# Row sums of the softmax in two attentions: added on GpSimd and VectorE instead of multiplied with ones on TensorE

## What is computed

```
q, k, v = (x_norm @ Wq.T + bq), (ctx @ Wk.T + bk), (ctx @ Wv.T + bv)     # split into 16 heads of 8
scores  = einsum('bhqd,bhkd->bhqk', q, k) / sqrt(8)                      # layer 1: rotated q and k
scores  = where(mask, scores, -inf or -1e9)                              # causal, or a given mask
probs   = softmax(scores, axis=-1)                                       # exp(s - max) / row sum
out     = einsum('bhqk,bhkd->bhqd', probs, v) @ Wo.T + bo
x       = x + tanh(gate) * out
```

## Time and profile before

| | us |
|---|---|
| median of three runs (lowest, highest) | 1851.87 (1851.81, 1856.1) |
| the profiled execution | 1866.66 |
| its span in the profile | 1864.9 |
| layer 1's attention, in the span | from 654 to 912 |
| layer 3's attention, in the span | from 1373 to 1639 |
| TensorE busy, whole span | 1600.8 (86%) |
| VectorE busy | 1219.1 (65%) |
| ScalarE busy | 1218.5 (65%) |
| GpSimd busy | 745.6 (40%) |

### The profile page before, as it was taken

The page is one execution under the profiler, slowest core; times in us unless marked ns, Lnnn a source line. Parts: engine busy times, 40 slices in busy tenths (PEclk is TensorE's granted clock), DMA queues, the critical chain, the costliest instruction groups (busy, mean ns, idle before and its releaser), DMA issues. The chain is left out here.

```text
span 1864.9 us, 38943 instructions
## 1 busy us (share of the span) xinstructions
PE 1600.8 (86%) x12723; PEld 1194.1 (64%) x12723; DVE 1219.1 (65%) x3299; ACT 1218.5 (65%) x4236; POOL 745.6 (40%) x719
## 2 busy tenths in 40 slices
PE   8399999699999699999699956999768999939994
PEld 6255555499999466666589855545545666626994
DVE  4699999688888577666567756212456777753444
ACT  3399999499999378778577743433247878822444
POOL 2355675245555421121068736001321334351452
PEclk9699999899999799999899977899779999966997
DMA  5320000300000124233190021200034453331224
GB/s 167 118 80 1 1 1 1 92 4 2 1 2 1 44 84 102 74 89 90 51 326 29 1 91 62 71 0 1 1 94 120 111 153 106 84 126 39 70 72 160
DMA packets 67239, 126.85 MB, mean 68 GB/s; under 512 B 11246, under 2 KB 29921, under 8 KB 65113
## 3 DMA queue, kind: packets, MB, share of 16 engines
q1 hardware_dynamic: 57338, 104.58, 19.8%
q10 hardware_dynamic: 5328, 11.01, 1.8%
q0 software_dynamic: 4384, 8.89, 1.4%
HBM read 90.91 MB, written 49.39 MB: 75 GB/s over the span
## 5 line engine op out<-in xcount | busy, mean ns | idle before, releaser
L1660 ACT ACTIVATE L_E<-L_sc,L_negm 128x128 f32<-128x128 f32 x1024 | 299.2, 402 | 112.8 <-DVE L_negm L1519 100.7
L616 ACT ACTIVATE B_E<-B_logits,B_m 128x32 f32<-128x32 f32 (+1 forms) x1792 | 362.6, 371 | 9.3 <-DVE B_m L585 8.2
L622 POOL TENSOR_TENSOR B_E<-B_E,B_r 128x512 f32<-128x512 f32 x256 | 267.5, 1046 | 230.5 <-DVE B_r L604 230.4
L1519 DVE TENSOR_REDUCE L_negm<-L_sc 128x4 f32<-128x512 f32 x256 | 174.6, 685 | 77.9 <-PE L_sc L1771 68.9
L585 DVE TENSOR_REDUCE B_m<-B_logits 128x16 f32<-128x512 f32 (+1 forms) x256 | 173.1, 676 | 38.6 <-PE B_logits L576 31.6
L1769 PE MATMUL L_sc<-KS,L_QS 128*128 128x512 f32 x256 | 141.7, 554 | 46.5 <-ACT L_E L1660 18.2
L599 DVE TENSOR_REDUCE B_r<-B_E 128x16 f32<-128x512 f32 (+1 forms) x256 | 172.6, 674 | 2.4 <-POOL B_E L622 1.3
L1668 ACT ACTIVATE L_PT<-L_pt 128x512 f32<-128x512 f32 x256 | 166.3, 651 | 0.5 <-PE L_pt L1779 0.5
L574 PE MATMUL B_logits<-B_phihi,B_xhi 128*128 128x512 f32 x256 | 154.0, 602 | 5.5 <-ACT B_E L616 2.7
L1779 PE MATMUL L_pt<-ident,L_E 128*128 128x128 f32 x1024 | 157.1, 277 | 0.8 <-ACT L_PT L1668 0.8
L1779 PEld LDWEIGHTS L_pt<-ident,L_E 128*128 128x128 f32 x1024 | 124.0, 142 | 22.9 <-issue 1.1
(11 more groups left out here) (360 smaller groups left out, 3566.9 us busy)
## 6 DMA issues: line engine op xcount, KB each, us to landing
route_rows<-in_F_fill SPq DMA_DIRECT2D x33, 516.0 KB, 19.8
KS<-L_ksplit SPq DMA_DIRECT2D x168, 64.0 KB
L_QS<-L_qsplit SPq DMA_DIRECT2D x42, 256.0 KB
F_xg<-route_rows SPq DMA_DIRECT2D x71, 64.5 KB
ew<-in_expert_w SPq DMA_DIRECT2D x1, 4096.0 KB, 17.2
L_cT<-in_ctxT SPq DMA_DIRECT2D x16, 256.0 KB, 4.7
F_w<-in_F_w SPq DMA_DIRECT2D x2, 2048.0 KB
F_yl<-F_y_rows SPq DMA_DIRECT2D x16, 256.0 KB, 5.8
```

Of the source, the lines that this page charges most:

```text
L616: ins = nc.scalar.activation(e[:, cols], self.bank(k)[:, cols], ACT.Exp, bias=self.m[:, k % 4, g:g + 1])
L622: self.st.nc.gpsimd.tensor_tensor(e, e, self.r[:, k % 2, :].unsqueeze(2) .to_broadcast([128, self.ng, self.size]), ALU.mult).then_inc(self ...
L1519: nc.vector.tensor_reduce(negm[:, k % 4, :], sc[k % 2][:].rearrange("p (h k) -> p h k", h=NHG), AX.X, ALU.max, negate=True).then_inc(s["ma ...
L1660: ins = nc.scalar.activation(e[:, h * 128:(h + 1) * 128], sc[k % 2][:, h * 128:(h + 1) * 128], ACT.Exp, bias=negm[:, k % 4, h:h + 1])
```

## The change

TensorE's four products with `OZ` per unit go, and `OZ` with them. In their place:

- `halve(k)`, GpSimd, even units: three additions that fold E's 128 keys a head to 64, 32 and 16 columns (outputs of 256, 128 and 64 columns), each waiting for the one before.
- `add_up(k-2)`, VectorE, right behind `maximum(k)`: for odd units a reduction of all of E (128 x 512), for even ones of the 64 folded columns. ScalarE's `exponent(k)` now also waits for `sum_done` of unit k-4.
- `invert(b)` moves to the head of unit 4b + 6: reciprocal of 128 x 16 sums and a copy that widens them to 128 x 128. `spread_sums(b)`, TensorE, one transpose in unit 4b + 7. `move_ratio(b)`, VectorE, copies it out of PSUM in unit 4b + 8, and `divide(b)` multiplies as before.
- GpSimd's order is written anew, unit by unit.

The diff, without the lines that only name tiles and semaphores:

```diff
@@ GpSimd
+            def halve(k):
+                e, i = E[k % 4][:].rearrange("p (h k) -> p h k", h=NHG), k // 2
+                g.wait_ge(s["exp_done"], k + 1)
+                nc.gpsimd.tensor_tensor(fold1[:], e[:, :, 0:64], e[:, :, 64:128], ALU.add).then_inc(s["half1"], 1)
+                g.wait_ge(s["half1"], i + 1)
+                nc.gpsimd.tensor_tensor(fold2[:], fold1[:, :, 0:32], fold1[:, :, 32:64], ALU.add).then_inc(s["half2"], 1)
+                g.wait_ge(s["half2"], i + 1)
+                if i >= 2:
+                    g.wait_ge(s["sum_done"], k - 3)
+                nc.gpsimd.tensor_tensor(fold3[i % 2][:], fold2[:, :, 0:16], fold2[:, :, 16:32], ALU.add)\
+                    .then_inc(s["folded"], 1)
...
             for n in range(NG):
-                scatter_between(n - 3, n, 1, range(2, 5))
-                if n + 1 < NG:
-                    split("k", n + 1)
-                scatter_between(n - 3, n, 3, range(5, 7))
-                if route and n >= 2:
-                    route.complete(g, n - 2)
-                if route:
-                    fold(n)
-                if n + 1 < NG:
-                    split("q", n + 1)
-                scatter_between(n - 3, n, 9, range(7, 8))
-                if n:
-                    tail.gpsimd(g, n - 1, (n - 1) % 2)
-                scatter_between(n - 2, n, UG - 1, range(2))
+                for w in range(UG):
+                    if w % 2 == 0:
+                        halve(n * UG + w)
+                    if w == 1:
+                        scatter_between(n - 3, n, 1, range(2, 4))
+                    if w == 2 and n + 1 < NG:
+                        split("k", n + 1)
+                    if w == 3:
+                        scatter_between(n - 3, n, 3, range(4, 6))
+                        if route and n >= 2 and n < 3:
+                            route.complete(g, n - 2)
+                    if w == 5:
+                        scatter_between(n - 3, n, 5, range(6, 8))
+                        if route and n >= 3:
+                            route.complete(g, n - 2)
+                        if route:
+                            fold(n)
+                    if w == 6 and n + 1 < NG:
+                        split("q", n + 1)
+                    if w == 14 and n:
+                        tail.gpsimd(g, n - 1, (n - 1) % 2)
+                    if w == 15:
+                        scatter_between(n - 2, n, UG - 1, range(2))
@@ VectorE
+            def move_ratio(b):
+                v.wait_ge(s["spread_done"], b + 1)
+                v.wait_ge(s["av_done"], NHG * (b + 1))
+                nc.vector.tensor_copy(ratio[b % 2][:], pp[b % 2][:, 128:256]).then_inc(s["ratio_moved"], 1)
+
+            def add_up(k):
+                b, hg = divmod(k, NHG)
+                if k % 2:
+                    v.wait_ge(s["exp_done"], k + 1)
+                    src = E[k % 4][:].rearrange("p (h k) -> p h k", h=NHG)
+                else:
+                    v.wait_ge(s["folded"], k // 2 + 1)
+                    src = fold3[k // 2 % 2][:]
+                if hg == 0 and b >= 2:
+                    v.wait_ge(s["inv_done"], b - 1)
+                nc.vector.tensor_reduce(rsum[b % 2][:, :, hg], src, AX.X, ALU.add).then_inc(s["sum_done"], 1)
+
             def invert(b):
-                v.wait_ge(s["av_done"], NHG * (b + 1))
-                nc.vector.reciprocal(rinv[b % 2][:], pp[b % 2][:, 128:256]).then_inc(s["inv_done"], 1)
+                v.wait_ge(s["sum_done"], NHG * (b + 1))
+                if b >= 2:
+                    v.wait_ge(s["spread_done"], b - 1)
+                nc.vector.reciprocal(rinv[b % 2][:], rsum[b % 2][:].rearrange("p c h -> p (c h)")).then_inc(s["inv_done"], 1)
+                v.wait_ge(s["inv_done"], b + 1)
+                nc.vector.tensor_copy(rwide[b % 2][:].rearrange("p (r d) -> p r d", d=HD),
+                                      rinv[b % 2][:].unsqueeze(2).to_broadcast([128, NHG * NHG, HD])).then_inc(s["widened"], 1)
...
-                nc.vector.tensor_tensor(OT[n % 2][:, cols], pp[b % 2][:, 0:128], rinv[b % 2][:], ALU.mult)\
+                nc.vector.tensor_tensor(OT[n % 2][:, cols], pp[b % 2][:, 0:128], ratio[b % 2][:], ALU.mult)\
...
-                    steps.link(nc.vector.memset(OZ[:], 0.0))
-                    steps.link(nc.vector.memset(diagonal(OZ[:], OZ[:].offset), 1.0))
...
+                    if k >= 6 and (k - 6) % NHG == 0:
+                        invert((k - 6) // NHG)
                     if due:
-                        invert(b)
+                        move_ratio(b)
...
                     maximum(k)
+                    if k >= 2:
+                        add_up(k - 2)
                     if due:
                         divide(b)
@@ ScalarE, exponent
                 if k >= 4:
                     a.wait_ge(s["pt_ready"], k - 3)
+                    a.wait_ge(s["sum_done"], k - 3)
@@ TensorE, attend
-                for at, weights in ((0, VZ[n % 2][:, j, :]), (128, OZ[:])):
-                    for c in range(NHG):
...
+                for c in range(NHG):
...
+            def spread_sums(b):
+                t.wait_ge(s["widened"], b + 1)
+                nc.tensor.transpose(pp[b % 2][:, 128:256], rwide[b % 2][:], p.ident[:]).then_inc(s["spread_done"], 1)
...
                         attend(k - ATTEND)
+                    if k >= 7 and k % NHG == 3:
+                        spread_sums(k // NHG - 1)
```

More of the change, by code:

```diff
@@ L1266, in stage_attn @@
         VZ = [st.sb(f"VZ{u}", [128, GB, NHG * 128]) for u in range(2)]
-        OZ = st.sb("OZ", [128, NHG * 128])
+        fold1, fold2 = st.sb("fold1", [128, NHG, 64]), st.sb("fold2", [128, NHG, 32])
+        fold3 = [st.sb(f"fold3{i}", [128, NHG, 16]) for i in range(2)]
+        rsum = [st.sb(f"rsum{i}", [128, NHG, NHG]) for i in range(2)]
         negm = st.sb("negm", [128, 4, NHG])
@@ L1270, in stage_attn @@
         PT = [st.sb(f"PT{i}", [128, 512]) for i in range(4)]
-        rinv = [st.sb(f"rinv{i}", [128, 128]) for i in range(2)]
+        rinv = [st.sb(f"rinv{i}", [128, NHG * NHG]) for i in range(2)]
+        rwide = [st.sb(f"rwide{i}", [128, 128]) for i in range(2)]
+        ratio = [st.sb(f"ratio{i}", [128, 128]) for i in range(2)]
         OT = [st.sb(f"OT{u}", [128, GD]) for u in range(2)]
@@ L1284, in stage_attn @@
             "q_split", "k_split", "q_put", "k_put", "q_taken", "k_taken", "q_sum", "k_sum", "q_hi", "k_hi",
-            "sc_ready", "max_ready", "exp_done", "pt_ready", "pt_moved", "av_done", "inv_done", "OT_ready", "v_ready", "const_ready", "zeroed", "VZ_zeroed", "QS_zeroed",
+            "sc_ready", "max_ready", "exp_done", "pt_ready", "pt_moved", "av_done", "inv_done", "half1", "half2", "folded", "sum_done", "spread_done", "ratio_moved", "widened", "OT_ready", "v_ready", "const_ready", "zeroed", "VZ_zeroed", "QS_zeroed",
             "wr_in", "w_folded", "w_diff")}
@@ L1529, in divide @@
                     v.wait_ge(s["aux_full"], turn_of["out", n - 2] + 1)
-                v.wait_ge(s["inv_done"], b + 1)
-                nc.vector.tensor_tensor(OT[n % 2][:, cols], pp[b % 2][:, 0:128], rinv[b % 2][:], ALU.mult)\
+                v.wait_ge(s["ratio_moved"], b + 1)
+                nc.vector.tensor_tensor(OT[n % 2][:, cols], pp[b % 2][:, 0:128], ratio[b % 2][:], ALU.mult)\
                     .then_inc(s["OT_ready"], 1)
@@ L1635, in _ @@
                     route_part(n - 2, w, 1)
-            for b in range(B - 2, B):
-                invert(b)
-                divide(b)
+            move_ratio(B - 2)
+            divide(B - 2)
+            add_up(NU - 2)
+            add_up(NU - 1)
+            invert(B - 1)
+            move_ratio(B - 1)
+            divide(B - 1)
             add_output(NG - 1)
@@ L1790, in attend @@
                 t.wait_ge(s["pt_moved"], k + 1)
-                for at, weights in ((0, VZ[n % 2][:, j, :]), (128, OZ[:])):
-                    for c in range(NHG):
[L1793 to L1796, removed]
+                for c in range(NHG):
+                    ins = nc.tensor.matmul(pp[b % 2][c * HW:(c + 1) * HW, 0:128],
+                                           VZ[n % 2][:, j, hg * 128 + c * HW:hg * 128 + (c + 1) * HW],
+                                           PT[k % 4][:, c * 128:(c + 1) * 128], start=(hg == 0),
+                                           stop=(hg == NHG - 1), skip_group_check=True)
                 ins.then_inc(s["av_done"], 1)
+            def spread_sums(b):
+                t.wait_ge(s["widened"], b + 1)
+                nc.tensor.transpose(pp[b % 2][:, 128:256], rwide[b % 2][:], p.ident[:]).then_inc(s["spread_done"], 1)
             if keyed:
@@ L1841, in _ @@
                     attend(k - ATTEND)
+                if k % NHG == 3:
+                    spread_sums(k // NHG - 1)
             if route:
```

## The result

The changed kernel takes 1908.11 us (median of four, 1906.73 to 1909.1); beside it the kernel before took 1851.84 (four runs, 1841.4 to 1856.1). The ratio is 1.0297, 95% interval 1.0264 to 1.033: slower by some 55 us. I had forecast slower, by 24, and the range ended at 1896. (A ratio leaves out an execution over 1.5% above the fastest of its kernel; here that changes only the run with the change in layer 1 alone.)

A forecast was written before the change was run, and what follows sets the result against it. TensorE leads, but ScalarE is level where no projection is added, and layer 1's edge waits for queries through DRAM. Layer 3's 14.8, 3.0 and 2.0, layer 1's 4.2 and -1.0, and 1.4 made +24.4 on 1851.9: 1876 us, range 1840 to 1896.

The forecast's parts named there:

- the two last batches: Each attention's last batch: sum, reciprocal, widening, transpose and copy replace one reciprocal, 0.7 us longer, twice: 1.4.
- TensorE's time buys nothing: Pairs without a projection gain 0.03 us, TensorE and ScalarE being level; the path sees 1.5 a group, taken as 1.0.
- The queue of GpSimd in layer 3: Groups 3 to 6: halving 6 ends at 1526.5 behind splits, scatters, `complete` and `fold`; unit 9's maximum starts 1.4 us late.
- I carry 1.2: Layer 3, groups 3 to 6: loss of 1.2 us a group from GpSimd's queue, some delay won back; bounds 0 and 2.5.
- I take 1.4: GpSimd's three dependent additions of one halving: 1.4 us together, between bounds of 0.92 and 1.65.
- The root in unit 15: Layer 3, groups 1 to 7: the root behind halving 14 delays `normalise` and the path by 2.5 us (2.0 to 3.1).
- I cost it at nothing there: VectorE's sums of odd units stand in a gap and cost nothing; without that cover 0.61 to 0.69 us each.
- 0.7 at the edge: Layer 1, six groups: halvings 2 and 6 delay k's and q's sums, 0.7 us an edge; bounds -1.0 and +1.9.
- Groups 1, 2 and 7 of layer 3: Groups 1 and 2: 2.5 us for the root less 1.0 gained, 3.0 together; group 7, without splits: 2.0.
- A: TensorE's time is the path and GpSimd keeps up: not slower, 1829, or 1840 for half the gain; chance 0.2.
- B: GpSimd's halvings and VectorE's two-input instructions shut each other out: 13 us more in layer 3, 4 in layer 1, 1893; chance 0.12.
- C: Gains and waits cancel within 0.3%, with low halving bounds in layer 3 and a gain at layer 1's edges: 1852; chance 0.1.

The follow-up runs named there:

- Experiment 5: Kernel before, with products with ones only in the first of a batch's four units and nothing added: 1849.57 against 1857.87 us, 0.9959.
- Experiment 3: Changed kernel with the inverse root ahead of halving 14, `complete` (from group 3) in unit 9 and `fold` in unit 11: 1883.26 us, 1.0159.
- experiment 9: Changed kernel with fourteen idle mask products on TensorE in layer 3's unit 15, ahead of its wait for the normalised rows: 1898.82 us, 1.0232.
- Experiment 4: Changed kernel without GpSimd's halvings; VectorE sums only the first 16 columns of each head in even units: 1863.86 us, 1.0043.
- experiment 11: Changed kernel with GpSimd's order moved: root before halving 14, `complete` and `fold` later, rotated parts added first: 1873.98 us, 1.0105.
- Experiment 10: Changed kernel with GpSimd adding layer 1's rotated parts of k and q ahead of halvings 2 and 6: 1890.39 us, 1.0198.

## Why the forecast was right in kind and wrong in size

The terms of my sum beside the profile (us; a group runs from mask product to mask product, group 7 to ScalarE's last `move`):

| term | forecast | profile |
|---|---|---|
| layer 3, groups 3 to 6 | 14.8 | 30.9 |
| layer 3, groups 1 and 2 | 3.0 | 6.3 |
| layer 3, group 7 | 2.0 | 7.6 |
| layer 3, group 0 | 0 | -2.4 |
| layer 1, groups 1 to 6 | 4.2 | 6.8 |
| layer 1, groups 0 and 7 | -1.0 | 4.7 |
| the two last batches (profile: last `move` to last division) | 1.4 | -2.4 |
| sum | 24.4 | 51.5 |

**TensorE's time buys nothing: right.** I set 0.03 us for pairs without a projection and at most 1.5 a group. Experiment 5 gives 4 us over both stages in the profile and 8 in the timing for 42 us of products; units 10 to 14, which carry no projection, take 9.1 us a group in layer 3 and 8.2 in layer 1 with them and without.

**The queue of GpSimd in layer 3: right in place, too small. This is the step that failed most.** It is the term "I carry 1.2", for each of groups 3 to 6; units 0 to 14 lost 4.2 us there. I put unit 9's maximum 20.3 us after the group's start, 1.4 later than before, and counted on part of the delay being won back; it started after 23.4 us, 4.5 later than before, and 4.2 of that was left at unit 15. The 3.1 us between forecast and measurement come from three places. The exponentials of unit 2 ended 1.1 us later than I said: unit 0 ran at half clock (2.87 us in place of 1.76). The queue from there to the end of halving 6 was 0.8 longer, with three halvings at 1.67 where "I take 1.4" (my high bound was 1.65). And I put the maximum of unit 9 straight behind the sum of unit 6, where the division and the four copies of v stand between them, 1.2 us, which VectorE did before in a gap and now does after the wait. Experiment 3 shows that this wait is real and apart from the root's.

**The root in unit 15: right, and 2.5 was 3.6.** `normalise` waited 2.4 us, and 2.8 was its delay against the exponentials of unit 14. Of the 0.8 left, experiment 9 puts 0.35 down to TensorE's clock (unit 15 from 6.70 to 6.35 us); the rest is open.

**The clock is a term that I had at nothing.** My sum took TensorE's rows at full speed. A wait of 3.8 us left TensorE at half speed for the units behind it. Experiment 9 takes the idling away and leaves the wait: 9 to 12 us in the timing, 5 in layer 3 of the profile, so a tenth to a fifth of the loss. Its price was in no row of before that I had read, though the clock of 0.98 in the earlier trace rows could have told me that there were such stretches.

**VectorE's new sums are another.** "I cost it at nothing there" was said of the sums of odd units. Experiment 4 has this work and no halvings; experiment 5 has neither, and keeps a quarter of the products. Layer 3 took 269.1 us in the one and 259.6 in the other, and the ratios are 1.0043 and 0.9959, with intervals that do not meet: some 9 us in layer 3 and 16 in all. This is an estimate from two kernels that differ in more than the sums; no run adds these alone. It is of the size of what experiment 11 leaves.

**Layer 1: right in cause, too small.** The step "0.7 at the edge", in groups 1 to 6, was 1.1; groups 0 and 7, for which I had a gain of 1.0, lost 3.3 and 1.4. The part I left out was ScalarE: its upper halves wait in line for GpSimd's sums, 14 us over the stage, and hold the exponentials up. Experiment 10 takes both away.

**Groups 1, 2 and 7 of layer 3.** I had 1.5 each for the first two; they lost 1.0 and 5.3. In group 2 `complete` stands in unit 3 and `fold` in unit 5, with the two first scatters behind: I had counted no queue there. Nor had I in group 7, which has no splits but all the rest: the sum of unit 6 waits 4.1 us there too (at 1669.94), and the group lost 7.6 where I had 2.0.

**The rivals.** A (TensorE is the path) fell with experiment 5. B (VectorE and GpSimd shut each other out) was not tried apart, but the traces bound it. VectorE's instructions in the two attentions exceed the median of their kind by 8.7 us in all before and by 17.2 after (counting those that do so by over 0.06 us); 7.5 of the 17.2 are the new widening copy, which took 0.23 us all 64 times without the halvings (experiment 4), and up to 0.68 with them, in 24 of 64. The product that took 1.91 us in the earlier trace rows has its like after (`R_oh`, 0.87 us at 1577.88, beside GpSimd's subtraction). So on VectorE's side B is at most 8.5 of the 54 us, less than its 13 + 4. C did not happen.

**The signs that I gave.** They held for the halvings' wait (2 to 4 us forecast, 4.1 measured), for ScalarE's idling ahead of `put_q` and for the root (2 and 2.4). Missed were layer 3 (15 to 25 us longer; 41 over the 266 named), layer 1 (within 5 of 258; 11.5 more) and TensorE's busy time: down by 45 us, I said. It fell by 24 over the whole kernel and by 8 in the two attentions, in part since its products ran at half clock more often.

## What to carry to other kernels

Before work is taken off the busiest engine, take a part of it away for nothing, as experiment 5 does: one run shows about what the whole change can bring, and here it was 0.4%, at most 0.8 by its interval, for three quarters of the work. An engine that is 30% busy, in a queue written in order, is free only where its gaps are; write down what stands ahead of the new instruction on its engine, and what stands behind the instruction that will wait for it on the other. When an item must be moved past new work, ask who waits for it: the root, the rotated sums and `complete` were each cheap, and their places cost 36 us.

## What the runs showed of the hardware

TensorE's clock answers to the kernel's own waits. The changed kernel has less TensorE work and longer gaps, and it ran its layer 3 at a mean granted clock of 0.90, with four transposes at 1.06 us in place of 0.60 behind a gap of 3.8 us. Less work alone did it too: experiment 5 adds nothing, and the clock lost in the two attentions rose from 9.7 to 17.0 us. Products whose result nobody reads, put into the gap of 3.8 us, made the kernel faster by 9 to 12 us, by intervals that just touch. The Trainium skill (TensorE: Matmul & The Clock Gate, "What's actually happening") says that the low clock is the resting state and activity lifts it; the two levels, and experiment 9, agree.

Three dependent additions on GpSimd of 256, 128 and 64 output columns take 0.73, 0.46 and 0.32 us, and 1.67 us from the first's start to the last's end: halving the width does not halve the price, and the waits between them add some 0.16.

GpSimd's additions lengthen a VectorE copy of 128 columns within SBUF: the widening copy took 0.23 us all 64 times in experiment 4, which has no halvings, and up to 0.68 in 24 of 64 in the changed kernel, as at 1581.27, beside the addition at 1581.12.
